# A graph network: the update network and the two normalisations after it, as one pipeline over chunks of four blocks

## What is computed

```python
    # second layer; msgs are the edge hiddens after the first ReLU
    agg = segment_sum(relu(msg_in @ mW1 + mb1) @ mW2 + mb2, dst) / clip(cnt, 1.0)[:, None]
    upd = relu(concatenate([h, agg], axis=-1) @ uW1 + ub1) @ uW2 + ub2
    upd = upd + h
    x = x + (upd - mean(upd)) * rsqrt(var(upd) + 1e-5) * gamma + beta
    h = relu(layernorm(x))
    # third layer
    support = h @ weight
    x = x + relu(segment_sum(edge_weight[:, None] * support[src], dst) + bias)
```

## Time and profile before

| | us |
|---|---|
| median of three runs | 5626.27 (5624.34 to 5633.94) |
| the profiled execution | 5629.7 |
| its span (first to last instruction) | 5627.9 |
| TensorE busy in the span | 4909.3 (87%) |
| VectorE | 3168.0 (56%) |
| ScalarE | 1754.6 (31%) |
| GpSimd | 2089.6 (37%) |

### The profile page before, as it was taken

The page is one execution under the profiler, slowest core; times in us unless marked ns, Lnnn a source line. Parts: engine busy times, 40 slices in busy tenths (PEclk is TensorE's granted clock), DMA queues, the critical chain, the costliest instruction groups (busy, mean ns, idle before and its releaser), DMA issues.

```text
span 5627.9 us, 139608 instructions
## 1 busy us (share of the span) xinstructions
PE 4909.3 (87%) x42810; PEld 4173.0 (74%) x42810; DVE 3168.0 (56%) x9378; ACT 1754.6 (31%) x3785; POOL 2089.6 (37%) x2575
## 2 busy tenths in 40 slices
PE   1899999998888888888888888659998999999998
PEld 1799999998777777777777777459996666666665
DVE  7899999996555555555555555630003444444444
ACT  2555555555111111111111111210001444445445
POOL 6211111111777777777777777000000111111000
PEclk8999999999999999999999999879998999999999
DMA  6344444444555555555555555037775554554554
GB/s 169 148 205 198 193 191 205 205 199 166 132 132 132 132 133 133 131 133 132 133 132 132 133 131 133 12 137 294 291 292 188 189 183 176 189 183 178 188 183 160
DMA packets 464598, 943.57 MB, mean 168 GB/s; under 512 B 107346, under 2 KB 395970, under 8 KB 426898
## 3 DMA queue, kind: packets, MB, share of 16 engines
q1 hardware_dynamic: 187778, 696.55, 32.9%
q0 software_dynamic: 58304, 121.69, 9.0%
q10 hardware_dynamic: 218448, 124.48, 8.2%
HBM read 691.90 MB, written 250.56 MB: 167 GB/s over the span
## 4 chain that ended last, share of the span: by engine, by line
PE 65%; issue 10%; POOL 9%; DVE 5%; DMA 4%; ACT 3%; DVEq 3%; ACTq 1%; POOLq 0%; SPq 0%
PE ps L1142 20%; PE ps L975 10%; PE ps L997 10%; POOL BIG L695 9%; PE ps L960 7%; PE ps L1075 4%; DMA BIG<-table,IDX 4%; PE ps L1073 4%; PE ps L1085 4%; PE ps L958 2%; DVEq L378 2%; PE ps L1074 1%; ACT ACC L805 1%; PE ps L1029 1%; DVE BIG L1482 1%
## 5 line engine op out<-in xcount | busy, mean ns | idle before, releaser
L695 POOL DMA_INDIRECT BIG<-table,IDX x1664 | 1615.9, 971 | 535.5 <-issue 470.3
L1491 DVE TENSOR_TENSOR ACC<-ACC,ps 128x257 f32 x1664 | 702.4, 422 | 588.9 <-PE ps L1085 571.1
L1073 PE MATMUL ps<-T,BIG 128*128 x3328 | 698.7, 293 | 342.0 <-DMA BIG<-table,IDX 194.5
L1073 PEld LDWEIGHTS ps<-T,BIG 128*128 128x128 f32 x3328 | 539.8, 200 | 458.0 <-issue 449.7
L1085 PE MATMUL ps<-BIG 128*128 128x257 f32 x3328 | 808.3, 385 | 0.0
L1075 PE MATMUL ps<-BIG,ident 128*128 128x128 f32 x3328 | 771.4, 315 | 0.0
L975 PE MATMUL ps<-H,ACC 128*128 128x128 f32 x4802 | 690.5, 284 | 0.0
L1085 PEld LDWEIGHTS ps<-BIG 128*128 128x128 f32 x3328 | 615.3, 195 | 73.6
L833 ACT ACTIVATE IDX<-SRC 128x4 int32 (+1 forms) x416 | 85.1, 205 | 1827.9 <-PE ps L1075 1144.3
L960 PE MATMUL ps<-T,BIG 128*128 128x98 bf16 x9408 | 633.0, 206 | 0.0
L958 PE MATMUL ps<-BIG 128*128 128x98 bf16 x3136 | 569.4, 207 | 70.1 <-ACT ACC L805 53.2
(11 more groups left out here) (233 smaller groups left out, 6318.9 us busy)
## 6 DMA issues: line engine op xcount, KB each, us to landing
weight_mat<-ACC SPq DMA_DIRECT2D x49, 3136.0 KB, 9.3
BIG<-weight_mat SPq DMA_DIRECT2D x49, 3136.0 KB, 10.2
BIG<-count_mat SPq DMA_DIRECT2D x73, 1568.0 KB, 6.5
REL_WT<-count_mat SPq DMA_DIRECT2D x72, 1568.0 KB, 6.6
count_mat<-BIG SPq DMA_DIRECT2D x49, 1568.0 KB, 12.8
BIG<-rel_tab ACTq DMA_DIRECT2D x416, 128.0 KB, 3.1
BIG<-in_edge_attr SPq DMA_DIRECT2D x832, 64.0 KB
BIG<-in_edge_attr ACTq DMA_DIRECT2D x832, 64.0 KB
```

The lines of the kernel that those rows point to most:

```text
L695: pool.indirect_dma_start(G[:, q * QUAD + u, :], None, tables[1], bass.IndirectOffsetOnAxis(ap=IDX[:, q, u:u + 1], axis=0)).then_inc(gathe ...
L1073: pe.matmul(to, DT[:, q % 2, u * P:(u + 1) * P], T1[:, b[q * QUAD + u], :], start=True, stop=False)
L1491: dve.tensor_tensor(to, to, PS[4 + u][:, 0:2 * F + 1], ALU.add).then_inc(slots_free, 1)
```

## The change

Everything from the mean of the hiddens to the product with Wg becomes one loop over 22 slots (C1 + 9), written out without hardware loops. Each body has a lag: in slot t it handles chunk t - lag, if there is one. So chunk 0 is turned in slot 0 and its support is copied out in slot 9, and in slots 9 to 12 all bodies run, each on another chunk. The order of bodies within a slot is fixed for each engine. Each turned or multiplied chunk has one PSUM bank of its own, instead of two banks in turn.

- Row sums times reciprocal count (one wide multiplication per chunk in place of four), ub2 onto H, the filling with the bias: now GpSimd. beta is added to X by GpSimd, instead of to T1 by VectorE.
- The normalisation of T1 (without gamma) is done by ScalarE with Identity and a scale and bias per row, in place of VectorE's subtract and multiply.
- Statistics are per chunk: bn_stats and bn_aggr for each block; Sqrt, reciprocal and nmr over the four columns of a chunk, twice per slot.
- WIN[0] and WIN[1] swap halves of BIG. Weight block 0 is loaded once uW2's product has been done for all chunks (it lies in T2), block 1 once Wg's product has (it lies in HT). The first count blocks are loaded when all 49 weight blocks are used up, one later than before.
- Elsewhere only the numbers change for which the semaphores wait.

The diff, cut to its core:

```diff
-        WIN = [BIG[:, k * NP:(k + 1) * NP] for k in range(2)]
+        WIN = [BIG[:, (1 - k) * NP:(2 - k) * NP] for k in range(2)]
...
+        UPDATE_SLOTS = C1 + 9
+        def slot(t, lag, body):
+            c = t - lag
+            if 0 <= c < C1:
+                body(c, CHUNK if c < CHUNKS else 1)
+        HT_PS = counts(C1, ("old", 0), ("new", 8))
+        ROWS = counts(0, ("mean", 0), ("h", 1), ("x", 3), ("bias", 8))
...
             def load_weights(base):
-                def body(b, par, i):
-                    sp.wait_ge(wsum_ps, base * BLOCKS + b + 1)
-                    sp.dma_start(WIN[par], weight_mat[b, :, :]).then_inc(wblk_in[par], 16)
-                block_pairs(sp, body)
+                sp.wait_ge(o_ps, C1)
+                sp.dma_start(WIN[0], weight_mat[0, :, :]).then_inc(wblk_in[0], 16)
+                sp.wait_ge(sup_ps, C1)
+                sp.dma_start(WIN[1], weight_mat[1, :, :]).then_inc(wblk_in[1], 16)
+                with sp.Fori(1, BLOCKS // 2) as i:
+                    for par in range(2):
+                        sp.wait_ge(wsum_ps, base * BLOCKS + (i * 2 + par + 1))
+                        sp.dma_start(WIN[par], weight_mat[i * 2 + par, :, :]).then_inc(wblk_in[par], 16)
...
-                sp.wait_ge(wsum_ps, 2 * BLOCKS + 1)
+                sp.wait_ge(wsum_ps, 2 * BLOCKS + 2)
                 load(0, 0, 0)
...
-            sp.wait_ge(sup_sb, C1 + 1)
             two_ways(sp, overfull, lambda: load_weights(1), lambda: general_table(T1, sup_sb, C1 + 1))
...
+            def mean_hidden(c, nb):
+                own = slice(c * CHUNK, c * CHUNK + nb)
+                pool.tensor_tensor(ACC[:, own, 0:F], ACC[:, own, 0:F], rcnt[:, own].rearrange("p (b a) -> p b a", a=1).broadcast_to([P, nb, F]),
+                                   ALU.mult).then_inc(s_ready, 1)
+            def h_plus(c, nb):
+                pool.wait_ge(hT_ps, HT_PS["old", c])
+                pool.tensor_tensor(blk(H, c, nb), blk(H, c, nb), wide("ub2", nb), ALU.add).then_inc(s_ready, 1)
+            def x_plus(c, nb):
+                pool.tensor_tensor(blk(X, c, nb), blk(X, c, nb), wide("beta", nb), ALU.add).then_inc(s_ready, 1)
+            def bias_init(c, nb):
+                pool.wait_ge(hT_ps, HT_PS["new", c])
+                pool.tensor_copy(blk(H, c, nb), wide("bias2g", nb)).then_inc(s_ready, 1)
+            pool.wait_ge(acc_ready, 4)
+            for t in range(UPDATE_SLOTS):
+                slot(t, 0, mean_hidden)
+                slot(t, 1, h_plus)
+                slot(t, 3, x_plus)
+                slot(t, 8, bias_init)
...
+            for t in range(UPDATE_SLOTS):          # ScalarE
+                slot(t, 5, std_of(lambda c: AGGR["t", c]))
+                slot(t, 7, std_of(lambda c: AGGR["x", c]))
+                slot(t, 0, h_turned)
+                slot(t, 0, s_turned)
+                slot(t, 2, agg_turned)
+                slot(t, 3, upd_hidden)
+                slot(t, 5, t_normed)
+                slot(t, 8, new_h_turned)
+                slot(t, 7, new_h)
...
+            for t in range(UPDATE_SLOTS):          # TensorE
+                slot(t, 0, turn_old_h)
+                slot(t, 0, turn_s)
+                slot(t, 1, times_w2)
+                slot(t, 9, times_wg)
+                slot(t, 8, turn_new_h)
+                slot(t, 2, turn_agg)
+                slot(t, 3, update)
+                slot(t, 4, times_u2)
...
+            def agg_out(c, nb):
+                dve.wait_ge(agg_ps, c + 1)
+                for j in range(nb):
+                    b = c * CHUNK + j
+                    last = dve.scalar_tensor_tensor(ACC[:, b, 0:F], bc["mb2"][:, :], cn[:, b:b + 1], PS[2][:, j * P:(j + 1) * P], ALU.mult, ALU.add)
+                last.then_inc(agg_sb, 1)
+            def upd_out(c, nb):
+                dve.wait_ge(o_ps, c + 1)
+                dve.wait_ge(s_ready, ROWS["h", c])
+                dve.tensor_tensor(blk(T1, c, nb), PS[5][:, 0:nb * P].rearrange("p (b f) -> p b f", f=F), blk(H, c, nb), ALU.add).then_inc(o_sb, 1)
+            def rstd_of(std):
+                def body(c, nb):
+                    own = slice(c * CHUNK, c * CHUNK + nb)
+                    dve.wait_ge(std_ready, std(c))
+                    link(dve.reciprocal(rstd[:, own], rstd[:, own]))
+                    dve.scalar_tensor_tensor(nmr[:, own], MV[:, own, 0], -1.0, rstd[:, own], ALU.mult, ALU.mult).then_inc(norm_ready, 1)
+                return body
+            def t_scaled(c, nb):
+                dve.wait_ge(std_ready, STD["t_normed", c])
+                marks["scaled", c] = marked(dve.tensor_tensor(blk(T1, c, nb), blk(T1, c, nb), wide("gamma", nb), ALU.mult))
+            def x_added(c, nb):
+                dve.wait_ge(link_done, marks["scaled", c])
+                dve.wait_ge(s_ready, ROWS["x", c])
+                marks["added", c] = marked(dve.tensor_tensor(blk(X, c, nb), blk(X, c, nb), blk(T1, c, nb), ALU.add))
...
+            for t in range(UPDATE_SLOTS):          # VectorE
+                slot(t, 5, rstd_of(lambda c: STD["t", c]))
+                slot(t, 7, rstd_of(lambda c: STD["x", c]))
+                slot(t, 1, agg_out)
+                slot(t, 6, t_scaled)
+                slot(t, 9, support_out)
+                slot(t, 6, x_added)
+                slot(t, 6, x_stats)
+                slot(t, 4, upd_out)
+                slot(t, 6, x_aggr)
+                slot(t, 4, t_stats)
+                slot(t, 4, t_aggr)
```

More of the change, by code:

```diff
@@ new lines, in upd_hidden, with t_normed @@
+            def upd_hidden(c, nb):
+                act.wait_ge(u_ps, c + 1)
+                act.activation(cols(T2, c, nb), PS[4][:, 0:nb * P], ACT.Relu, bias=ub1c[:, 0:1]).then_inc(u_sb, 1)
+            def t_normed(c, nb):
+                act.wait_ge(norm_ready, NORM["t", c])
+                for b in range(c * CHUNK, c * CHUNK + nb):
+                    last = act.activation(T1[:, b, :], T1[:, b, :], ACT.Identity, bias=nmr[:, b:b + 1], scale=rstd[:, b:b + 1])
+                last.then_inc(std_ready, 1)
@@ new lines, in new_h, with new_h_turned @@
+            def new_h(c, nb):
+                act.wait_ge(norm_ready, NORM["x", c])
+                for b in range(c * CHUNK, c * CHUNK + nb):
+                    last = act.activation(H[:, b, :], X[:, b, :], ACT.Relu, bias=nmr[:, b:b + 1], scale=rstd[:, b:b + 1])
+                last.then_inc(h_ready, 1)
+            def new_h_turned(c, nb):
+                act.wait_ge(hT_ps, HT_PS["new", c])
+                act.activation(cols(HT, c, nb), PS[6][:, 0:nb * P], ACT.Copy).then_inc(hT_sb, 1)
@@ new lines, in times_u2, with turn_new_h @@
+            def times_u2(c, nb):
+                pe.wait_ge(u_sb, c + 2)
+                pe.wait_ge(o_sb, c + 1)
+                for j in range(nb):
+                    mm = pe.matmul(PS[5][:, j * P:(j + 1) * P], T2[:, bass.ds((c * CHUNK + j) * P, P)], uW2s[:, :], start=True, stop=True)
+                mm.then_inc(o_ps, 1)
+            def turn_new_h(c, nb):
+                pe.wait_ge(h_ready, 2 * C1 + c + 1)
+                pe.wait_ge(hT_sb, HT_SB["new", c - 1] if c else HT_SB["old", 0])
+                for j in range(nb):
+                    mm = pe.transpose(PS[6][:, j * P:(j + 1) * P], H[:, c * CHUNK + j, :], ident[:, :])
+                mm.then_inc(hT_ps, 1)
@@ new lines, in times_wg @@
+            def times_wg(c, nb):
+                pe.wait_ge(hT_sb, HT_SB["new", c])
+                pe.wait_ge(sup_sb, c + 1)
+                for j in range(nb):
+                    mm = pe.matmul(PS[7][:, j * P:(j + 1) * P], HT[:, bass.ds((c * CHUNK + j) * P, P)], Wgs[:, :], start=True, stop=True)
+                mm.then_inc(sup_ps, 1)
+            for t in range(UPDATE_SLOTS):
[7 more added lines that the diff above has]
+                slot(t, 4, times_u2)
@@ new lines, in t_scaled, with x_stats @@
+            def t_scaled(c, nb):
[5 more added lines that the diff above has]
+                marks["added", c] = marked(dve.tensor_tensor(blk(X, c, nb), blk(X, c, nb), blk(T1, c, nb), ALU.add))
+            def x_stats(c, nb):
+                dve.wait_ge(link_done, marks["added", c])
+                for b in of_chunk(c, nb):
+                    last = dve.bn_stats(ST[:, b, :], X[:, b, :])
+                marks["x", c] = marked(last)
```

200 lines of the change are left out of this document (104 added, 96 removed).

## The result

The changed kernel takes 5540.24 us (median of 4 runs, 5538.11 to 5542.21), the kernel before 5626.3 in runs on the same chip: a ratio of 0.9847, 95% interval [0.9835, 0.9858], or 86 us less. Forecast were 71 less, 5555, with 5540 as the low end of the range. So sign and mechanism were right and the size was 15 us short; the time lies 0.2 us inside the range.

What follows compares the result with a forecast made beforehand. No engine was full; they took turns over 199.5 us of stage and bare DMA. Fill 19, slots and drain 99.5, port waits 10 and 0.3 to the product make 128.8, 71 us earlier: 5555, range 5540 to 5592.

Steps and rivals of the forecast that it cites:

- the loads: Weight blocks 0 and 1 ahead of the dense product: issued earlier, both land in time, removing 10.2 us of bare DMA.
- Fill: First slots of the pipeline, where GpSimd brings the means and TensorE is late: 19 us.
- VectorE sets the slots: Full slots 9 to 12: VectorE's 8.2 us is the longest, against ScalarE 6.4 and TensorE 7.1; slots last 8.2 to 9.5.
- VectorE's own sum of a full slot: Slots 9 to 12: VectorE's steps sum to 7.8 us, with the start after the Sqrt 8.2 us.
- Port waits: VectorE's two-SBUF-input steps wait out GpSimd instructions: 1.1 us a full slot (0 to 4.4), 10 us over twelve slots.
- the ring: Loop through TensorE and ScalarE from turn_new_h over update, Relu, t_normed and copy to new_h: 7.6 us a slot.
- Dense product to count product: Count loads leave one block later, but the first count product's wait for VectorE covers it by 4.9 us: cost 0.
- Rival 1: GpSimd or ports decide the stage: port waits 53 us, giving 5598, or additions of 3.4 us, giving 5590; chance 0.14.
- Rival 2: TensorE's clock falls to 1.2 GHz in the stage: 180 us, saving 20, giving 5606; chance 0.05.
- Rival 3: ScalarE's Identity needs its own table: slots 1 to 2 us longer, saving 53, giving 5573; inside the 0.74 main case.
- Rival 4: VectorE and GpSimd exclude each other wholly, additions 3.4 us: full slot 19, stage 246, 5672; chance 0.04 with intermediate cases.
- Rival 5: Drain under 10 us leaves the rest of weight block 0 bare, 10 us at most: 5565; inside the 0.74 main case.

## Why the prediction was right, and where its size was off

**The bound of before, the one-for-one gain behind it, the loads.** Right. The gain in the stage came out at the end; the forward loads gave the 10.2 that they were counted at, alone (10.2) and undone (10.4, of which 0.7 lay in the slots).

**Fill.** Forecast 19 us, measured 20.2. Right to 6%.

**VectorE sets the slots.** Right, by the idle time and by one engine's added work at a time (6.1, 0.9 and 1.3 us ahead of the drain). The sign given for it, full slots of 8.2 to 9.5 us, held for two of four.

**VectorE's own sum of a full slot.** This is the term that was mis-sized: 8.2 forecast, 6.8 measured. Slot 12 of the changed kernel, with 0.06 of port waits, lasts 6.86. From start to start in the kernel without reads by GpSimd, the parts add up to 6.81 (forecast in brackets): two reciprocal and nmr pairs 0.58 (0.76), agg_out 1.04 (1.08), t_scaled 0.60 (0.61), support_out 0.60 (0.66), x_added 0.71 (0.68), x_stats 0.79 (0.96), upd_out 0.59 (0.66), x_aggr 0.29 (0.6), t_stats 0.87 (1.0), t_aggr 0.38 (0.6), own waits in these (0.15), the Sqrt's gap 0.36 (0.4). The two aggregations are 0.53 of the 1.35 too much and the two statistics 0.30. One aggregation alone lasts 182 ns, four in a run take 0.38: I had allowed for such overlap and not enough. Over slots 5 to the end 84.6 us are left for the forecast's 99.5, once fill and port waits are taken from 112.5.

**Port waits.** Forecast 10 us (0 to 53), measured 7.7 of waits, by the mechanism named; without them the last upd_out came 5.5 earlier, not 7.7, since the ring is then the bound. Not foreseen: nearly two thirds (5.1) fall on nmr, an instruction of 0.16 us that waits out what is left of a GpSimd addition (up to 1.11 us in all), and most of the waits come in four slots (8 to 11, 7.7 to 8.3 us each).

**The sum.** 128.8 forecast for the stage: +1.2 fill, -14.9 slots, -2.3 ports, -0.3 ahead of the product: 112.5. The saving of 86 is that of the range's low end, but not for its reasons: there the ports cost nothing and the fill was 5 less, and here they cost 7.7 and it was 1.2 more. That the time still fell inside the range, by 0.2 us, is luck. So is the quick return of the clock in the changed kernel's drain; the slow kind costs 2.7. Two working steps don't hold: ScalarE's parts of the ring (0.63, 1.55, 0.52 and 1.55) are 4.25, not 4.4, and the ring is 7.4 by these rows, not 7.6, and the 3.4 us for an addition in rivals 1 and 4 doesn't follow from 0.841 for 256 columns, which makes 1.7 for 512. Neither enters the sum.

**Dense product to count product.** Cost forecast at 0, "that wait covers it by 4.9". The cover held: no DMA wait. The 2.0 us came from a wait on VectorE itself that no row of before showed.

**The rivals.** Rival 1: additions took 1.04 to 1.39 us and the ports 7.7, far from 53. Rival 2: the clock was 1.00 in full slots; what runs at 1.2 GHz throughout, in some runs, is the drain, at 2.7 us of cost. Rival 3: Identity rows stand among Sqrt and Relu without a table load. Rival 4: a slot never came near 16.5. Rival 5: block 0 had 15.65 us to land. The order of the row sums, which cost 37 us when they stood on VectorE in the wrong slot, wasn't among the rivals: the kernel that falls into it differs from one with a stage of 116.7 us by the place of one body.

## What to carry to other kernels

In a pipeline written out over several engines, ask of each pair of engines whether both wait for the other within one slot; putting one producer a slot earlier was worth 37 us here, where the move of 26 us of VectorE's work to another engine was worth 4. When work goes to GpSimd beside a VectorE that sets the pace, count what VectorE waits for its reads, small two-input instructions first: these waits were 7.7 us here, against a gain that was small anyhow, since VectorE had idle time to take the work. And size a stream of short VectorE instructions from the distance between starts in a run of them, not from the duration of a lone one.

## What was not expected of the hardware

- A GpSimd instruction that only writes SBUF delays no VectorE instruction with two SBUF inputs (162 ns against 375 for nmr, with GpSimd busy about as long).
- VectorE stops for 2.6 to 4.0 us with no releaser behind the start of large loads. The stall was absent in the three pipelines with 13 or 52 more VectorE instructions ahead of that place, and in the one with later loads. Its cause stays open.
- TensorE's clock comes back to 2.4 GHz within the drain in six of the twelve pipelines' traces and not in the other six. It did in the changed kernel's and not in that of the kernel with later count loads, though the two have the same compute instructions in the stage and start the last upd_out within 0.2 us of each other. What decides it stays open; each kernel has one trace. The slow kind costs 2.7 us, as much as several of the edits tried here are worth; so a gain in the middle must be read at a point ahead of the drain.
